# Holding row loads, spreading pad stores and moving scatters of the last sequence pair in a Mamba and mixture-of-experts kernel

## What is computed

```
h = layernorm(x) * (1 + ca) + sa
x = x + ga * mamba2(h)                      # projections, causal convolution, state scan, norm, projection
h = layernorm(x) * (1 + cb) + sb
gout = h @ Wg.T ; top 2 of 8 experts, softmax over the two
expert e: eo = (silu(h W1[e].T + b1[e]) * (h W2[e].T + b2[e])) W3[e].T + b3[e]
x = x + gb * (sum over the two experts of weight * eo)
```

## Time and profile before

| what | value |
|---|---|
| median of 3 runs | 822.5 us (821.74 to 823.63) |
| the profiled execution, its own time | 832.36 us |
| its span, first to last instruction | 830.5 us |
| PE busy / DVE / ACT / POOL | 82% / 67% / 62% / 56% of the span |
| mean granted TensorE clock | 0.916 of full speed |
| DMA traffic | 88.86 MB, mean 107 GB/s |

### The profile page before, as it was taken

The page is one execution under the profiler, slowest core; times in us unless marked ns, Lnnn a source line. Parts: engine busy times, 40 slices in busy tenths (PEclk is TensorE's granted clock), DMA queues, the critical chain, the costliest instruction groups (busy, mean ns, idle before and its releaser), DMA issues. The chain is left out here.

```text
span 830.5 us, 13734 instructions
## 1 busy us (share of the span) xinstructions
PE 680.6 (82%) x3713; PEld 518.9 (62%) x3713; DVE 559.4 (67%) x1640; ACT 516.8 (62%) x1223; POOL 462.0 (56%) x366
## 2 busy tenths in 40 slices
PE   3678899789789999998999999999966952774982
PEld 3246557556567776876787777768755731553662
DVE  2827967988986997898689978987743561231421
ACT  3784795896796899687969977886522310221320
POOL 2003004444453378757775786688687477357775
PEclk9779798999998999999999999999996967897997
DMA  5100001112013465455346444653645774857973
GB/s 186 28 0 1 1 27 32 45 52 71 33 58 102 119 168 129 105 155 125 92 105 174 107 97 103 204 104 90 180 107 120 200 204 95 202 123 149 191 169 28
DMA packets 81275, 88.86 MB, mean 107 GB/s; under 512 B 7360, under 2 KB 67696, under 8 KB 81200
## 3 DMA queue, kind: packets, MB, share of 16 engines
q1 hardware_dynamic: 54528, 61.37, 25.6%
q0 software_dynamic: 26672, 26.62, 18.0%
HBM read 54.50 MB, written 33.46 MB: 106 GB/s over the span
## 5 line engine op out<-in xcount | busy, mean ns | idle before, releaser
L457 POOL DMA_INDIRECT out<-xs x142 | 226.8, 1597 | 116.9 <-issue 53.2
L427 POOL DMA_INDIRECT rows<-payload,pos x128 | 131.6, 1028 | 68.2 <-issue 30.2
L880 DVE SCALAR_TENSOR_TENSOR xbc<-T,table,xbc 128x511 f32<-128x511 f32 (+2 forms) x192 | 141.9, 746 | 7.7 <-ACT xbc L599 3.1
L1133 DVE SCALAR_TENSOR_TENSOR xs<-FX,xs 128x128 f32<-128x128 f32 x142 | 43.1, 345 | 122.6 <-PE FX L1457 104.7
L1457 PE MATMUL FX<-wt,hid 128*128 128x128 f32 x568 | 87.8, 301 | 17.2 <-DVE hid L1125 17.2
L655 ACT ACTIVATE xt<-FX 128x256 f32<-128x256 f32 x71 | 27.0, 380 | 110.1 <-PE FX L1434 96.0
L1457 PEld LDWEIGHTS FX<-wt,hid 128*128 128x128 f32 x568 | 73.7, 203 | 26.6 <-DVE hid L1125 17.9
L648 ACT ACTIVATE sg<-FG,wt 128x256 f32<-128x256 f32 x142 | 59.3, 471 | 47.0 <-PE FG L1444 38.4
L1444 PE MATMUL FG<-xt,wt 128*128 128x256 f32 x284 | 77.6, 397 | 12.1 <-DMA wt<-in_wt 8.1
L1287 PE MATMUL T<-h,win 128*128 128x512 f32 x128 | 76.7, 698 | 12.4 <-DVE xbc L880 10.6
L1444 PE MATMUL FV<-xt,wt 128*128 128x256 f32 x284 | 78.2, 400 | 0.0
(11 more groups left out here) (207 smaller groups left out, 1343.5 us busy)
## 6 DMA issues: line engine op xcount, KB each, us to landing
wt<-in_wt SPq DMA_DIRECT2D x71, 386.0 KB
xs<-rows SPq DMA_DIRECT2D x71, 258.0 KB
x<-in_x SPq DMA_DIRECT2D x8, 512.0 KB, 4.3
out<-x SPq DMA_DIRECT2D x8, 512.0 KB
out<-xs POOLq DMA_INDIRECT x142
rows<-pad SPq DMA_DIRECT2D x8, 258.0 KB
rows<-payload,pos POOLq DMA_INDIRECT x128
gate_a<-gates SPq DMA_DIRECT2D x8, 128.0 KB, 4.3
```

Source lines behind the costliest of these rows:

```text
L427: pool.indirect_dma_start(d["rows"], bass.IndirectOffsetOnAxis(ap=pos[:, k, n:n + 1], axis=0), payload[:, n, :], None).then_inc(scattered, 16)
L457: pool.indirect_dma_start(d["out"], bass.IndirectOffsetOnAxis(ap=xs[:, t % XSR, c, PAY - 1:PAY].bitcast(U32), axis=0), xs[:, t % XSR, c, 0 ...
L880: last = nc.vector.scalar_tensor_tensor(out=xbc[:, t, k, tap:L], in0=T[:, k, 0:L - tap], scalar=w, in1=xbc[:, t, k, tap:L], op0=ALU.mult, ...
```

## The change

Five things. (a) For tiles 33 to 51, `load_rows(t)` waits until the addition of t-5 has landed, for 52 and 53 until that of t-6 has; for all others t-7 stays (`reach`). (b) The pad stores go in pairs behind rows 45, 46, 47 and 48, and their row numbers are computed at the end of `rows(7)` instead of in `new_tiles(7)`. (c) Weights 49, 50 and 51 are loaded ahead of rows 49. (d) POOL's order for the last pair becomes: additions 38, 39, scatters 0 and 1, addition 40, scatter 2, addition 41, scatter 3, addition 42, second weight, scatter 4, addition 43, scatter 5, addition 44, scatter 6, addition 45, scatter 7, addition 46. A scatter here is two DMAs. (e) On PE the turn of tile 49 stands behind the down product of 48. The other seven calls of `load_weights` in the loop change as the one shown.

```diff
--- before.py
+++ after.py
@@ -42,6 +42,7 @@
 DUMP = E * REGION + FIRST
 XR = 3
 WR, XSR = 4, 7
+AHEAD = 3
 DOWN = 2 * FT * P
 B12 = DOWN + FT * D
 WT = B12 + 2 * FT
@@ -297,6 +298,14 @@
                 e = sp_.value_load(tile_e[0:1, t:t + 1], min_val=0, max_val=E - 1)
                 sp_.dma_start(wt[:, t % WR, :], d["wt"][bass.ds(e, 1), :, :].rearrange("o p n -> p (o n)")).then_inc(wt_in[t % WR], 16)
 
+            def load_weights_of(t):
+                if not 0 <= t - (NTILES - LAST) < AHEAD:
+                    load_weights(t)
+
+            def reach(t):
+                n = t - (NTILES - LAST)
+                return XSR if n < -2 * PT or n >= AHEAD + 2 else XSR - 2 if n < AHEAD else XSR - 1
+
             def set_pads_of(e):
                 r = sp_.value_load(pad_row[0:1, e:e + 1], min_val=0, max_val=DUMP)
                 sp_.dma_start(d["rows"][bass.ds(r, TR), :].rearrange("(c p) m -> p c m", p=P), pad[:, :, :]).then_inc(pads_set, 16)
@@ -307,15 +316,19 @@
                 if t == 0:
                     sp_.wait_ge(dump_set, 32)
                 if t == NTILES - LAST:
-                    sp_.wait_ge(pads_ready, 1)
-                    for e in range(E):
-                        set_pads_of(e)
+                    for n in range(AHEAD):
+                        load_weights(t + n)
                 if t >= NTILES - LAST:
                     sp_.wait_ge(pads_set, 16 * E)
                 sp_.wait_ge(scattered, 16 * 2 * J * (p + 1))
-                landed(sp_, t - XSR)
+                landed(sp_, t - reach(t))
                 r = sp_.value_load(tile_row[0:1, t:t + 1], min_val=0, max_val=DUMP + TR)
                 sp_.dma_start(xs[:, t % XSR, :, :], d["rows"][bass.ds(r, TR), :].rearrange("(c p) m -> p c m", p=P)).then_inc(xs_in[t % XSR], 16)
+                n = t - (NTILES - LAST) + E // 2
+                if 0 <= n < E // 2:
+                    sp_.wait_ge(pads_ready, 1)
+                    set_pads_of(2 * n)
+                    set_pads_of(2 * n + 1)
 
             load_x(0)
             for dst, src in ((table[:, :], "table"), (wmod, "wmod"), (wout, "wout")):
@@ -336,28 +349,28 @@
...
                 if is_tile(PT * i - 29):
-                    load_weights(PT * i - 29)
+                    load_weights_of(PT * i - 29)
...
@@ -457,6 +470,15 @@
                     pool.indirect_dma_start(d["out"], bass.IndirectOffsetOnAxis(ap=xs[:, t % XSR, c, PAY - 1:PAY].bitcast(U32), axis=0),
                                             xs[:, t % XSR, c, 0:D], None, compute_op=ALU.add).then_inc(added[t % 2], 16)
 
+            def last_scatters(p):
+                t = PT * (p + 1) - 24
+                scatter(p, 0)
+                for n in range(6):
+                    scatter(p, n + 1)
+                    add_out(t + n)
+                    if n == 2:
+                        second_weight(p)
+
             for i in range(-2, 13):
                 if is_pair(i - 2):
                     scatter(i - 2, 7)
@@ -469,6 +491,9 @@
                     weight_by_decay(i, 2)
                 if is_tile(PT * i - 25):
                     add_out(PT * i - 25)
+                if i == NP:
+                    last_scatters(i - 1)
+                    continue
                 if is_tile(PT * i - 24):
                     add_out(PT * i - 24)
                 if is_pair(i - 1):
@@ -1070,6 +1095,9 @@
                 nc.vector.tensor_scalar(payload[:, :, 2 * D], tanh[:, :], 0.5, 0.5, ALU.mult, ALU.add)
                 nc.vector.tensor_scalar(payload[:, :, 2 * D + 1].bitcast(U32), part["token"], float(p * 2 * L), None, ALU.add)
                 nc.vector.tensor_copy(pos[:, :, :], posf[:, :, :]).then_inc(pos_ready, 1)
+                if p == NP - 1:
+                    link(nc.vector.tensor_tensor(out=pad_from[:, :], in0=cum[:, :], in1=part["region"], op=ALU.add))
+                    nc.vector.tensor_copy(pad_row[:, :], pad_from[:, :]).then_inc(pads_ready, 1)
 
             def split_b3():
                 vec.wait_ge(b3_in, 16)
@@ -1086,9 +1114,7 @@
                     link(nc.vector.tensor_tensor(out=full[:, :, :], in0=wide(cum[:, :], KT),
                                                  in1=part["steps"].unsqueeze(1).to_broadcast([P, E, KT]), op=ALU.is_ge))
                 else:
-                    nc.vector.tensor_tensor(out=pad_from[:, :], in0=cum[:, :], in1=part["region"], op=ALU.add)
                     link(nc.vector.tensor_scalar(cum_up[:, :], cum[:, :], float(TR), None, ALU.add))
-                    nc.vector.tensor_copy(pad_row[:, :], pad_from[:, :]).then_inc(pads_ready, 1)
                     link(nc.vector.tensor_tensor(out=full[:, :, :], in0=wide(cum_up[:, :], KT),
                                                  in1=part["steps"].unsqueeze(1).to_broadcast([P, E, KT]), op=ALU.is_gt))
                 link(nc.vector.tensor_reduce(out=tiles_of[:, :], in_=full[:, :, :], axis=AX.X, op=ALU.add))
@@ -1584,12 +1610,14 @@
                 if is_pair(i + 1):
                     turn_y(i + 1, 0)
                     intra(i + 1, 1)
-                if is_tile(PT * i - 15):
+                if is_tile(PT * i - 15) and PT * i - 15 != NTILES - LAST:
                     expert_turn(PT * i - 15)
                 if is_pair(i):
                     turn_h2(i)
                 if is_tile(PT * i - 16):
                     expert_down(PT * i - 16)
+                if PT * i - 15 == NTILES - LAST:
+                    expert_turn(PT * i - 15)
                 if is_pair(i + 1):
                     new_state(i + 1, 2)
                 if is_tile(PT * i - 15):
```

More of the change, by code:

```diff
@@ L338, in _ @@
                 if is_tile(PT * i - 29):
-                    load_weights(PT * i - 29)
+                    load_weights_of(PT * i - 29)
                 if is_tile(PT * i - 28):
-                    load_weights(PT * i - 28)
+                    load_weights_of(PT * i - 28)
                 if is_tile(PT * i - 26):
@@ L344, in _ @@
                 if is_tile(PT * i - 27):
-                    load_weights(PT * i - 27)
+                    load_weights_of(PT * i - 27)
                 if is_tile(PT * i - 26):
-                    load_weights(PT * i - 26)
+                    load_weights_of(PT * i - 26)
                 if is_tile(PT * i - 25):
                     load_rows(PT * i - 25)
-                    load_weights(PT * i - 25)
+                    load_weights_of(PT * i - 25)
                 if is_pair(i - 1):
@@ L354, in _ @@
                     load_rows(PT * i - 24)
-                    load_weights(PT * i - 24)
+                    load_weights_of(PT * i - 24)
                 if is_pair(i + 2):
@@ L359, in _ @@
                     load_rows(PT * i - 23)
-                    load_weights(PT * i - 23)
+                    load_weights_of(PT * i - 23)
                 if is_tile(PT * i - 22):
@@ L369, in _ @@
                 if is_tile(PT * i - 22):
-                    load_weights(PT * i - 22)
+                    load_weights_of(PT * i - 22)
             sp_.wait_ge(x1_stored, 16 * NP)
```

## The result

The changed kernel takes 829.81 us (median of 15 runs, 826.53 to 833.22) against 824.04 us (821.17 to 828.75) for the kernel before in the same session. The ratio is 1.0056, with a 95% interval of 1.0036 to 1.0075: slower by 0.56%, some 4.6 us (the two medians lie 5.8 us apart). The forecast was 821.2 us where the kernel before had 822.5: 0.16% faster.

What follows compares the result with a forecast made beforehand. POOL's additions and the waits for their landings were taken to bound the kernel. +1.0 at addition 46 and -2.3 after it gave -1.3, so 822.5 becomes 821.2 us; own range 818.5 to 824, with rivals 814 to 828.

Steps and rivals of the forecast that it cites:

- Step (1): Row loads held in pass 7: wait behind addition 31 falls from 6.02 to 4.3 us, -1.7 (bounds 0 and -1.8).
- Steps (2) to (4): Additions 40 to 46: scatters go first, rows 45 await landing 40, weights 43 and output 45 come late; +1.0 at 46.
- rival A: With weights 43 and 44 early, POOL sets the pace and it is faster: 819.3 to 811.7 us; chance 0.20.
- Step (5): Spread pads: issues of 1.24 us each on SP between 664 and 695, landing long before the last scatter.
- Step (6): Weights 49 to 51 ahead of rows 49: not in their way; rows leave at 707.9 instead of 706.94, load hidden.
- Step (7): Serial additions 46 to 50: fewer row loads at once shorten the waits, -2.3 us (bounds 0 and -6.4).
- Step (8): After addition 50 nothing changes: 88.5 us to the last issue.
- B: Last pair: late weights 37 push the wo product past 620.2, so positions come late; 824.9, up to 828 us; chance 0.22.
- C: Held bytes only move; spacings 46 to 50 and the wait behind 31 stay: 823.5 to 825.2 us; chance 0.13.
- The clock: PE at FG of 43 runs at the lower clock after waiting some 10 us; 2 us added before the list of tiles.

Runs made afterwards that it cites:

- e3: Changed kernel with the same hold, but weights 34 to 39 and 42 to 48 ahead of the held rows on SP; ratio 0.9938.
- f4: e3 with weights 58 and 66 also ahead of the row loads that stood in front of them; ratio 0.9992.
- g1: e3 timed once more, unchanged; ratio 0.9914.
- g2: Kernel before plus new POOL order, three weights ahead of rows 49, turn of 49 later, hold for 33 to 40 with weights 34 to 39 first; 0.9989.
- h3: Changed kernel with the weight order of e3, hold for tiles 33 to 40 and 49 to 53 but not 41 to 48; ratio 0.9927.
- f2: Kernel before with only the new order of scatters and additions on POOL; ratio 0.9976.
- e1: Changed kernel without the hold, every row load waiting for t-7 again; ratio 0.9987.
- g3: Changed kernel with the hold for tiles 33 to 40 alone; ratio 0.9928.
- h4: g3 timed once more, unchanged; ratio 0.9973.
- f1: e3 with the hold taken away, weights still first; ratio 0.9985.
- e4: Changed kernel with the hold kept for tiles 49 to 53 alone; ratio 0.9979.
- h2: Changed kernel with the first two pad stores behind weights 43 and 44 instead of ahead; ratio 1.0050.
- e2: Kernel before with only the hold on the row loads, tiles 33 to 53; ratio 1.0046.

## Why the prediction was wrong, point by point

**Step (1), hold in pass 7: -1.7, measured -0.4 at the positions.** The wait behind addition 31 fell as forecast, from 6.02 to 4.35 us (578.83 to 583.18). The hold does this in every profile: 4.1 to 4.5 us in the eleven kernels that have it for tiles 33 to 40, 5.4 to 7.0 in the seven without. But in the changed kernel the gain ended one addition later. Weights 34 left 5.6 us after a31 and not 0.6 ahead of it, and weights 35 to 37 left 11 us later than before, both counted from a31, where I had them 2 to 5 us late for PE. FG of 34 waited 2.22 us and took 2.07 (that of 35, at 595.21, took 1.07), the down product of 33 stands behind it on PE, and addition 33 waited for output 33. I had priced weights 35 to 37 by the cover of the wo product and never asked what weights 34 hold. In the five kernels with this hold where they come first (e3, f4, g1, g2, h3) addition 33 follows a31 by 14.3 to 14.7 us (before 16.2, after 16.1) and the residual by 35.9 to 36.5 (before 37.7, after 38.0): there the 1.7 is nearly whole. At the positions it is blurred again, 66.5 to 68.2.

**Steps (2) to (4), the mechanism: right.** Four scatters stand ahead of addition 40; rows 45, two pads and weights 43 leave in a row; PE is idle 9.09 us ("some 10"); FG of 43 is at pos + 21.1 (forecast + 19.8); the list of tiles at pos + 32.5 (+ 31.1), output 45 at pos + 47.8 (+ 46.6).

**Their size: the term that failed.** The sum of steps (1) to (4) at addition 46 was +1.0; counted from a31 it measured +5.3. Of what lies between, 1.3 us are the gain at the positions that did not come, and 3.1 come behind them. Behind the positions I had pos + 53.8 against + 51.1 before. It was + 56.9. Of the 3.1 us missing, 1.2 are output 45, late by that much more. The rest is POOL's: addition 45 comes 1.9 behind the end of output 45 and waits for landing 44 (1.76 us, named DMA), where I had only the issue, 0.8; and 46 follows in 7.12 us, not 6.39. By the program it too waits for a landing, that of 45, though its row names the issue (1.06). I had taken output 45 as the last of all waits and left out the landings. From the second issue to the next addition that is 5.93 us for 45 (691.70 to 697.63) and 5.21 for 46 (699.54 to 704.75), where the quiet wait is 4.20. The additions start late and close together, beside the rows, weights and pads that were let go together with them; whether that is the cause, no run shows.

And the comparison was with the wrong thing. Where tiles 41 to 48 are not held, the new order on POOL has addition 46 at pos + 47.2 to + 50.1 (f2, e1, g3, h4, f1, e4, g2; h3, with + 51.6, is the exception), 1 to 4 us sooner than before. I had that gain as rival A, conditional on early weights, and counted its loss nowhere, since I priced the hold against the old order. The hold takes 8.6 us in the profiles at this point (e1 to after). Against the kernel before, the timed runs show no gain of the order by itself (e1, f2), so this is a loss of places in the profile more than of time.

**Step (5), pads: right** that they are cheap; h2 moved the two that I named, with 2.5 us on FG of 43 and none on the time that can be told. **Step (6): right**; rows 49 left at pos + 58.8, addition 50 did not wait for weights.

**Step (7), additions 46 to 50: -2.3, measured -3.1, and mostly not by the hold.** I credited fewer row loads at once. The four spacings were 7.25, 6.09, 7.52 and 7.28 us, forecast 6.5, 6.8, 9.0 and 6.68. Only the second follows the hold: 47 to 48 takes 6.0 to 6.4 us in the nine profiles with rows 49 to 53 held and weights 49 to 51 ahead, 6.6 to 7.9 in the seven without that hold, and 8.12 before. The whole stretch gains about 1 us by it, 27.4 to 28.7 us against 27.4 to 29.6, and e4 against e1 shows none of that in the time. e2, with the hold but the pads in one block, takes 33.4, at a DMA share of 0.61 over 702 to 715 us: a low share alone doesn't make the additions quick. The 31.3 that I began from is longer than in any other kernel but e2, and was probably long in that one execution. Of the forecast gain little was there to be had; this made the sum negative.

**Step (8): right**, 86.0 after 86.6.

**The rivals.** B's number came true (824.9, up to 828, on 822.5: +0.3% to +0.7%) and its place did not, so that is luck. The wo product ended late, 37.7 us after a31 (616.56) where before it ended at 31.9. That is 5.8 us, more than the 4.2 that I allowed, but with no earlier POOL its cover was 5.9 and just held: the residual starts at 38.0, before at 37.7. And g3 and h4, which have that hold alone, are not slower. C is not seen in the profile: the wait behind 31 and the spacings both fell. A's condition, early weights, is met in e1 and f2; addition 46 comes sooner there, and the time hardly moves.

**The clock.** The trace has FG of 43 at 2.07 us after 9.09 us without work, where it took 1.06 before. In the same trace FG of 34 and of 42 took 2.07 after 2.22 and 4.71 us of waiting for weights, and FG of 37 took 1.34 after 2.73; the product with wo behind it took 3.74, and not the 7.4 that rival B has for it. I had put 2 us for FG of 43 and what follows it; from FG of 43 to the list took 11.4 us, before 9.4. The term was right, and it was the small part of the loss.

What stays open: what the hold of 33 to 40 alone gives. g3 and h4 are both below 1, but g3 has the positions early (65.8, in one long execution) and h4 has not (68.7); and e1, the same kernel without it, is 0.9987 with an interval that overlaps h4's. Nor is it settled whether the hold gains once the weights are first: e3, g1 and h3 (0.9914 to 0.9938) say so against f1 (0.9985), and f4 (0.9992) and g2 (0.9989) do not.

## What to carry to other kernels

Before a load is made to wait for a semaphore, list what stands behind it on the same queue, and price the first of these that an engine needs, then the next; put the loads that other engines wait for ahead of the held one (one order of the same instructions was 1.0056, another 0.9938 and 0.9914). Make the sum between two profiles from a common point of unchanged work, and don't count a gain on a stretch that only one execution shows to be long. And a part that gains under a condition has to be lost in the sum when another part breaks that condition.

## What the runs showed of the hardware that was not expected

The length of PE's idle time ahead of the chain from the last pair's residual to its positions did not set what that chain takes. Behind the residual PE's first eight matmuls take 2.07 to 2.08 us in all 18 profiles, after gaps of 3.98 (the changed kernel) to 13.44 us; the gap is 13.44 us in e1 and 5.74 in h4. PE in e1, then in h4:

```profile
621.65 2.08 PE L1483 MATMUL FX<-wt,hid 128*128 128x128 f32 x8 [13.44 <-DVE hid L1151]
623.52 1.91 PE L1470 MATMUL FV<-xt,wt 128*128 128x256 f32 x4
...
630.65 1.62 PE L1483 MATMUL FX<-wt,hid 128*128 128x128 f32 x8
```

```profile
621.59 2.08 PE L1483 MATMUL FX<-wt,hid 128*128 128x128 f32 x8 [5.74 <-DVE hid L1151]
623.46 1.91 PE L1470 MATMUL FV<-xt,wt 128*128 128x256 f32 x4
...
630.71 2.08 PE L1483 MATMUL FX<-wt,hid 128*128 128x128 f32 x8
```

Both take 2.08 us for eight matmuls that take 1.16 further on (at 636.23 in e1, at 637.21 in h4), and e1, with the longer gap, needs 30.4 us for the stretch (616.10 to 646.54), h4 31.5 (616.02 to 647.53). What differs in these rows is the second burst: after 2.88 us of idle its eight matmuls take 1.62 us in e1, after 3.63 us 2.08 in h4. e3 and g1, one program with gaps of 7.2 and 7.6 us, need 30.4 and 31.6. The busy time by stretch (its columns as above) has the clock at 0.75 in e1 and 0.78 in h4:

```profile
616.10:646.50 30.40, 21.20 (x111) 17.63 (x111) 14.46 (x77) 9.89 (x23) 20.38 (x15) 0.75 0.63 152
```

```profile
616.00:647.50 31.50, 21.50 (x111) 18.25 (x111) 14.49 (x77) 10.16 (x24) 20.52 (x15) 0.78 0.61 147
```

Of the 18 profiles 17 need 30.4 to 31.7 us for this stretch. The one of g3 needs 26.4, at a granted clock of 0.87, and the rows show where it starts to gain. DVE has the variance for norm 2 (L851) and POOL computes its power (L398), in h4:

```profile
620.55 0.17 DVE L851 TENSOR_TENSOR var<-within,apart 128x8 f32<-128x8 f32 x1
...
624.97 1.68 POOL L398 TENSOR_TENSOR rstd<-var,table 128x8 f32<-128x8 f32 x1
```

and in g3:

```profile
632.95 0.17 DVE L851 TENSOR_TENSOR var<-within,apart 128x8 f32<-128x8 f32 x1
...
634.58 1.68 POOL L398 TENSOR_TENSOR rstd<-var,table 128x8 f32<-128x8 f32 x1
```

In 17 profiles POOL starts the power 4.1 to 4.3 us after the variance is there, because it is still issuing an addition and a scatter; in g3, where the residual comes latest after a31 (39.4 us), it is through with them after 1.5. So 2.8 us of the way to the positions is a place in POOL's order. No run moved the power ahead of those issues; that it would pay is not shown.

The other surprise is how far two executions of unchanged work lie apart: 5.3 us over the first 580 in the two profiles, 14 us over all 18 (a31 at 574.9 to 589.0), and 826.5 to 833.2 us over 15 runs of the changed kernel. The same program timed twice gave 0.9938 and 0.9914 (e3, g1), and 0.9928 and 0.9973 (g3, h4).
